# A written-out order for four engines: the pieces of one batch round stand in another order

## The reference

```python
# layer 0 and layer 2: chunks of 64 columns, 8 heads of 16, keys = queries' source = ctx
out = chunk_attn(ctx, ctx, ctx, mask, W_in, b_in, W_out, b_out) + x
x   = (out - mean(out)) * rsqrt(var(out) + eps)          # over the row
# layer 1: 32 heads of 32 with 8 key/value heads, low-rank additions to every weight
x   = hidden + attention(hidden=x, traces=ctx)           # 128 rows x 128 keys
# layer 3: first three rows of the context are coordinates
idx = top_k(2 p.p - |p|^2 - |p|^2, 30)                   # 1024 x 1024 distances per batch
rel = pts[idx] - pts                                     # gathered neighbours
h   = three small layers with batch norm over all batches, on (rho, theta, phi) of rel
x   = x + sum_k softmax(h)_k * x[idx_k]
```

## Time and profile before

| | us |
|---|---|
| median of 3 runs | 6556.02 (6547.49 to 6559.64) |
| the profiled execution, its own time | 6548.45 |
| its span, first to last instruction | 6546.7 |
| PE busy in the span | 6073.3 (93%) |
| DVE busy | 5841.3 (89%) |
| ACT busy | 4481.8 (68%) |
| POOL busy | 3099.7 (47%) |
| mean granted TensorE clock | 0.965 of full |

### The profile page before, as it was taken

One profiled execution on the slowest core, in us unless ns is written; L12 is line 12 of the kernel. 1 busy time (PEld: TensorE's weight loads), 2 busy tenths in 40 slices (PEclk: granted clock), 3 DMA queues, 4 the chain that ended last, 5 costly groups with the idle time before them and its releaser, 6 DMA issues.

```text
span 6546.7 us, 207457 instructions
## 1 busy us (share of the span) xinstructions
PE 6073.3 (93%) x79430; PEld 4398.2 (67%) x79430; DVE 5841.3 (89%) x8381; ACT 4481.8 (68%) x10453; POOL 3099.7 (47%) x3527
## 2 busy tenths in 40 slices
PE   8999999999999999999999999999999795999999
PEld 4666666666666666666666666666666333888888
DVE  6999999999999999999999999999998678888887
ACT  4777777667777776777677777666776146777776
POOL 3555555555555555555555555555555200333221
PEclk9999999999999999999999999999999897999999
DMA  4222222222222222222222222222223303322222
...
DMA packets 301388, 499.07 MB, mean 76 GB/s; under 512 B 103858, under 2 KB 217698, under 8 KB 299682
## 3 DMA queue, kind: packets, MB, share of 16 engines
...
## 4 chain that ended last, share of the span: by engine, by line
PE 58%; DVE 19%; issue 11%; DMA 5%; ACT 3%; POOL 2%; DVEq 0%; SPq 0%; POOLq 0%; ACTq 0%
PE PD L1183 7%; PE PD L718 5%; PE MISC L743 5%; DVE pd L1768 4%; PE SCB L1169 4%; PE SCA L1169 4%; DVE m L1758 4%; DMA gat<-low_scratch 4%; PE TP L904 3%; PE SCA L938 3%; DVE idx L1764 3%; DVE gat L1711 3%; PE TP L911 2%; PE TP L790 2%; PE SCB L815 2%
## 5 line engine op out<-in xcount | busy, mean ns | idle before, releaser
L1758 DVE MAX8 m<-pd 128x8 f32<-128x1024 f32 x1024 | 1234.0, 1220 | 121.0 <-issue 45.3
L1764 DVE FIND_INDEX8 idx<-m,pd 128x8 uint32<-128x1024 f32 x1024 | 1245.7, 1219 | 5.8 <-issue 5.6
L545 POOL TENSOR_TENSOR prod<-prod,hm 128x480 f32<-128x480 f32 x384 | 416.3, 1084 | 1255.7 <-ACT prod L1373 1224.0
L1768 DVE MATCH_REPLACE8 pd<-m,pd 128x1024 f32<-128x1024 f32 x768 | 927.3, 1209 | 0.0
L743 PEld LDWEIGHTS MISC<-ptab,gat 128*128 128x128 bf16 x23400 | 638.4, 97 | 242.3 <-DVE gat L1711 137.0
L1253 ACT ACTIVATE pd<-PD,xxcol 128x512 f32<-128x512 f32 x514 | 354.8, 690 | 636.5 <-PE PD L719 464.1
L743 PE MATMUL MISC<-ptab,gat 128*128 128x24 bf16 x23400 | 654.3, 174 | 119.7 <-DVE gat L1711 119.2
L2070 DVE TENSOR_TENSOR gat<-maskT,con 120x2048 f32<-120x2048 f32 x256 | 581.5, 2302 | 123.4 <-PE SCB L1169 97.5
L1352 ACT ACTIVATE S<-SCB,mx 128x64 f32<-128x64 f32 (+1 forms) x2560 | 590.4, 368 | 78.9 <-DVE mx L1780 78.9
L718 PE MATMUL PD<-arena 128*128 128x512 f32 x1028 | 558.8, 626 | 49.5 <-ACT pd L1253 44.4
L1352 ACT ACTIVATE S<-SCA,mx 128x64 f32<-128x64 f32 (+1 forms) x2560 | 585.5, 415 | 12.7 <-DVE mx L1780 12.1
(11 more groups left out here) (274 smaller groups left out, 14397.3 us busy)
## 6 DMA issues: line engine op xcount, KB each, us to landing
gat<-low_scratch SPq DMA_DIRECT2D x396, 640.0 KB, 4.0
...
```

The lines of the kernel that those rows point to most:

```text
L1758: V.max(m, buf[:, :]).then_inc(found, 1)
L1764: last = V.max_index(idx[:, t, 8 * r:8 * r + 8], m, buf[:, :])
L1768: V.match_replace(buf[:, :], m, buf[:, :], -3.0e38).then_inc(found, 1)
```

## The change

In `rounds(i)` of PE, ACT, DVE and POOL the same pieces stand in another order; SP's list is as it was. No piece is added or taken out, only the eleven steps of the searches are cut at other places. The diff, cut to its core (POOL and DVE whole, PE and ACT their beginnings and ends):

```diff
--- before.py
+++ after.py
@@ -610,26 +610,26 @@
 
 pool.wait_ge(split_ready, i + 1)
 consume(i, 0)
-consume(i, 1)
-consume(i, 2)
 sides(i, 0)
 sides(i, 1)
+consume(i, 1)
 sides(i, 2)
 sides(i, 3)
+blend(0, X1)
+consume(i, 2)
 consume(i, 3)
-blend(0, X1)
+tangents(i, 0)
 consume(i, 4)
 consume(i, 5)
-tangents(i, 0)
 consume(i, 6)
 consume(i, 7)
 consume(i, 8)
 blend(1, X0)
 tangents(i, 1)
+turn(i)
+norm_parts(i + 1)
 consume(i, 9)
 consume(i, 10)
-turn(i)
-norm_parts(i + 1)
 consume(i, 11)
 indices()
 table()
@@ -940,128 +940,128 @@
     if h:
         last.then_inc(oproj_ready, 1)
 
+keys(0)
+distance(i, 1, 0, (pd_evac, i * 16 + 2))
+queries(0)
 chunk_values(0)
-keys(0)
-queries(0)
-split(i)
-distance(i, 1, 0, (pd_evac, i * 16 + 2))
-turn_context()
 distance(i, 1, 1, (pd_evac, i * 16 + 3))
 scores(0, 0)
 scores(0, 1)
-fill(i, 0, MISC)
 x3_half(i, 0, (pd_evac, i * 16 + 4))
+split(i)
+x3_half(i, 1, (tab_done, i * 2 + 1))
+turn_context()
 turn_probs(0, 0)
 turn_probs(0, 1)
+distance(i, 2, 0, (tab_done, i * 2 + 2))
+scores(0, 2)
+weigh(0, 0)
+fill(i, 0, MISC)
+weigh(0, 1)
+turn_probs(0, 2)
+turn_probs(0, 3)
 fill(i, 1, MISC)
-weigh(0, 0)
-weigh(0, 1)
-x3_half(i, 1, (tab_done, i * 2 + 1))
-scores(0, 2)
-turn_probs(0, 2)
-fill(i, 2, MISC)
-outputs(0)
-turn_probs(0, 3)
-distance(i, 2, 0, (tab_done, i * 2 + 2))
 weigh(0, 2)
 weigh(0, 3)
-fill(i, 3, MISC)
 scores(0, 3)
+outputs(0)
+distance(i, 2, 1, (pd_evac, i * 16 + 5))
 turn_probs(0, 4)
 turn_probs(0, 5)
-distance(i, 2, 1, (pd_evac, i * 16 + 5))
+fill(i, 2, MISC)
 weigh(0, 4)
+weigh(0, 5)
+outputs(1)
+turn_probs(0, 6)
 queries(1)
-turn_probs(0, 6)
-weigh(0, 5)
 turn_probs(0, 7)
-outputs(1)
 outputs(2)
-full_values()
 weigh(0, 6)
 weigh(0, 7)
-full_keys()
+full_values()
 outputs(3)
 distance(i, 3, 0, (pd_evac, i * 16 + 6))
 project(0)
+full_keys()
+chunk_values(1)
+distance(i, 3, 1, (pd_evac, i * 16 + 7))
+fill(i, 3, MISC)
...
-fill(i, 10, MISC)
-turn_probs(2, 5)
-turn_probs(2, 6)
-norms(i + 1, 0, (pd_evac, i * 16 + 16))
-turn_probs(2, 7)
 weigh(2, 4)
 weigh(2, 5)
+norms(i + 1, 0, (pd_evac, i * 16 + 16))
 weigh(2, 6)
+norms(i + 1, 1, (xx_evac, i * 3 + 4))
 weigh(2, 7)
-norms(i + 1, 1, (xx_evac, i * 3 + 4))
-fill(i, 11, MISC)
 outputs(10)
+norms(i + 1, 2, (xx_evac, i * 3 + 5))
 outputs(11)
-norms(i + 1, 2, (xx_evac, i * 3 + 5))
+fill(i, 10, MISC)
 project_full(0)
 project_full(1)
+fill(i, 11, MISC)
 distance(i + 1, 0, 0, (xx_evac, i * 3 + 6))
 distance(i + 1, 0, 1, (pd_evac, i * 16 + 17))
 
@@ -1422,133 +1422,133 @@
     act.wait_ge(v_ready, i * 2 + 2)
     act.dma_start(ctx[:, :], ctx_in[(i + 1) % NB, :, :]).then_inc(ctx_ld, 16)
 
-value_evacuate(0)
 key_evacuate(0)
 expand(0, 0)
+distance(i, 1, 0)
+expand(0, 1)
+query_evacuate(0)
+distance(i, 1, 1)
+value_evacuate(0)
+expand(0, 2)
+x3_half(i, 0)
 split_evacuate(i)
-distance(i, 1, 0)
-query_evacuate(0)
-expand(0, 1)
-distance(i, 1, 1)
-expand(0, 2)
 exponentials(0, 0)
 exponentials(0, 1)
+x3_half(i, 1)
+evict(0, 0)
+evict(0, 1)
+context_evacuate()
+exponentials(0, 2)
+exponentials(0, 3)
 pick(0)
-evict(0, 0)
-context_evacuate()
-evict(0, 1)
-x3_half(i, 0)
-exponentials(0, 2)
-pick(1)
-exponentials(0, 3)
-x3_half(i, 1)
+expand(0, 3)
 evict(0, 2)
-expand(0, 3)
 evict(0, 3)
-pick(2)
+distance(i, 2, 0)
 exponentials(0, 4)
 exponentials(0, 5)
-distance(i, 2, 0)
-output(0)
+pick(1)
 evict(0, 4)
 evict(0, 5)
+output(0)
 exponentials(0, 6)
 exponentials(0, 7)
 evict(0, 6)
+output(1)
+store_rows()
 evict(0, 7)
-store_rows()
+output(2)
 distance(i, 2, 1)
-pick(3)
-output(1)
...
 angles(act, i)
+norms(i + 1, 2)
 output(10)
 output(11)
+pick(10)
 pick(11)
-norms(i + 1, 2)
 distance(i + 1, 0, 0)
 deviation(1)
 distance(i + 1, 0, 1)
@@ -1819,88 +1819,100 @@
 
 search(0, 0, 1)
 mask_bias()
-search(0, 1, 8)
+search(0, 1, 4)
+search(1, 0, 1)
+search(0, 4, 5)
 front(0, 0)
+search(0, 5, 6)
+search(1, 1, 2)
 front(0, 1)
+search(0, 6, 7)
+search(1, 2, 3)
+search(0, 7, 9)
 onehot(i, 0)
 onehot(i, 1)
-search(0, 8, 10)
-search(1, 0, 2)
 onehot(i, 2)
-search(1, 2, 3)
+search(1, 3, 4)
+search(0, 9, 11)
+front(0, 2)
+normalise(0)
+search(1, 4, 5)
+normalise(1)
+front(0, 3)
+search(1, 5, 8)
+normalise(2)
+search(1, 8, 11)
+search(2, 0, 1)
+normalise(3)
+search(2, 1, 3)
 onehot(i, 3)
-normalise(0)
-front(0, 2)
-search(1, 3, 6)
-search(0, 10, 11)
 onehot(i, 4)
+search(2, 3, 4)
 onehot(i, 5)
-front(0, 3)
-search(1, 6, 8)
-normalise(1)
-search(1, 8, 9)
-normalise(2)
-search(1, 9, 10)
-search(2, 0, 4)
-search(1, 10, 11)
-normalise(3)
-search(2, 4, 6)
+search(2, 4, 7)
+moments(X1)
+scaled(0)
+search(2, 7, 10)
+search(3, 0, 1)
 onehot(i, 6)
-search(2, 6, 11)
-moments(X1)
-search(3, 0, 1)
-scaled(0)
-search(3, 1, 4)
+search(2, 10, 11)
 front(1, 0)
-search(3, 4, 7)
+search(3, 1, 6)
 front(1, 1)
-divide(i)
-search(3, 7, 8)
+search(3, 6, 7)
+search(4, 0, 1)
+search(3, 7, 9)
+search(4, 1, 3)
+front(1, 2)
+search(4, 3, 4)
+search(3, 9, 10)
+search(4, 4, 6)
+search(3, 10, 11)
+normalise(4)
+search(4, 6, 7)
 onehot(i, 7)
 onehot(i, 8)
-search(4, 0, 2)
-search(3, 8, 9)
-search(4, 2, 3)
-front(1, 2)
-search(4, 3, 6)
-normalise(4)
-search(4, 6, 7)
-search(3, 9, 11)
-search(4, 7, 9)
+onehot(i, 9)
 front(1, 3)
 normalise(5)
-onehot(i, 9)
-search(4, 9, 11)
+search(4, 7, 8)
+normalise(6)
+search(4, 8, 9)
+divide(i)
+search(4, 9, 10)
 onehot(i, 10)
+search(4, 10, 11)
 front(2, 0)
-search(5, 0, 4)
-normalise(6)
+search(5, 0, 1)
+front(2, 1)
 normalise(7)
-search(5, 4, 6)
-onehot(i, 11)
-front(2, 1)
+search(5, 1, 7)
 front(2, 2)
-search(5, 6, 9)
-search(6, 0, 1)
+search(5, 7, 9)
+front(2, 3)
 search(5, 9, 10)
 normalise(8)
 search(5, 10, 11)
 normalise(9)
-front(2, 3)
-search(6, 1, 4)
-search(7, 0, 3)
+search(6, 0, 2)
+onehot(i, 11)
+search(6, 2, 4)
 normalise(10)
+search(7, 0, 1)
 normalise(11)
-search(7, 3, 5)
+search(7, 1, 4)
 search(6, 4, 6)
-search(7, 5, 9)
-search(6, 6, 7)
-search(7, 9, 10)
-search(6, 7, 11)
-search(7, 10, 11)
+search(7, 4, 6)
+search(6, 6, 8)
+search(7, 6, 7)
+search(6, 8, 10)
+search(7, 7, 8)
+search(6, 10, 11)
 full_residual()
 moments(X0)
+search(7, 8, 9)
 scaled(1)
+search(7, 9, 11)
 assert chain[0] == DVE_STEPS, chain[0]
 
             with dve.Fori(0, NB // 2) as pair:
```

149 lines of the change are left out of this document (75 added, 74 removed).

## The result

The changed kernel takes 6583.64 us (median of 6 runs, 6564.88 to 6607.20), the kernel before 6557.09 us (6 runs, 6547.49 to 6563.20): a ratio of 1.0046, 95% interval 1.0032 to 1.0060. It is slower, by 27 us from median to median and by 30 us by the ratio, where 26 us faster were forecast. The time lies inside the range, near its upper end, and the sign is wrong.

What follows compares the result with a forecast made beforehand. The prediction took DVE to bound a round, PE nearly as close. Its terms summed to -0.9 us a round, -29 us over 32, with 3 us added for the ends: -26 us, 6556 to 6530 us; range 6478 to 6590.

Steps and rivals of the forecast that it cites:

- Term 1: VectorE's searches: ten fewer largest-eight or taking-out steps directly followed by a dependent one, at 0.23 us: -2.3 us a round.
- Term 2: Round's end: a search step covers 0.7 us of waits, but scaled(1) waits about 0.7 us after ScalarE's table load: 0.
- Terms 3 and 4: One-hots: 0 to 2 wait and stretch more, +0.8 us a round; the later ones fall in POOL's gaps, -0.8 us.
- Term 5: Waits of 1.3 us at moments(X1) instead of 0.5, +0.8 us a round, and at scaled(0), +0.4 us.
- Term 6: Small stalls at front(2, 0) and normalise(7), where PE and DVE meet within 0.3 us: +0.2 us a round.
- against a round without the turn of the loop: Basis of the walk: per-round effects reckoned on a round without a loop turn, summing to -0.9 us, times 32.
- DVE is the bound of a round, with PE and the chains some microseconds behind: Whole round: DVE bounds it, 145.3 us of DVE and 146.2 us of PE; PE and ACT/POOL chains some microseconds behind.
- The second rival: Turn of the round: PE becomes the bound if its waits are 2 us more than 4.3: +38, 6594 us; chance 0.20.

Runs made afterwards that it cites:

- Experiment 3: Kernel before, only the searches' steps dealt out anew, 29 dependent neighbours down to 16: 6577.98 us, 1.0034.
- 1: Changed kernel with the first steps of search(1) put back behind those of search(0) in VectorE's list: 6584.22 us, 1.0039.
- 9: Changed kernel with TensorE's split and ScalarE's split_evacuate put forward, behind distance(i, 1, 1) and its copy: 6551.46 us, 0.9989.
- 10: Kernel of 9 with VectorE's first steps of search(1) a little later, 20 dependent neighbours instead of 19: 6537.31 us, 0.9959.
- 11: Changed kernel with four rounds to a turn of the loop instead of two: 6547.82 us, 0.9987.
- 12: Kernel before with four rounds to a turn of the loop instead of two: 6530.76 us, 0.9952.
- 6: Kernel before with project_full summing 6 of its 8 parts, 3.6 us less TensorE time a round: 6529.22 us, 0.9957.
- 17: Kernel before with three unread products ahead of chunk_values(0) at the head of each TensorE round: 6650.82 us, 1.0158.
- 5: Changed kernel with project_full summing 6 of its 8 parts, 3.6 us less TensorE time a round: 6555.51 us, 1.0005.
- experiment 15: Changed kernel with a milder split move, later first search(1) steps, and search(2, 7, 8) between moments(X1) and scaled(0): 6580.83 us, 1.0040.
- experiment 13: Kernel of 10 with five unread products ahead of split(i) on TensorE, where it waited for GpSimd: 6637.48 us, 1.0124.

## Why the prediction was wrong, by its own steps

*Term 1, ten dependent neighbours fewer: right.* The idle time ahead of an index step's load, in both kernels (before first):

```profile
L1764 DVE MATCH_VALUE_LOAD idx<-m,pd 128x8 f32 x992 | 84.4, 85 | 88.2 <-DVE m L1758 8.2
```

```profile
L1764 DVE MATCH_VALUE_LOAD idx<-m,pd 128x8 f32 x984 | 81.6, 83 | 42.2 <-DVE m L1758 7.6
```

46 us in 31 rounds, 0.15 us for each of the ten, and the 0.09 us by which an independent instruction starts before the largest-eight step has ended. Experiment 3, with 13 fewer, has it in whole rounds: the shortest takes 150.8 us, before 153.1; 13 at 0.23 us would be 3.0.

*Term 2, the end of the round:* right, `scaled(1)` waits 0.74 us in the row; forecast 0.7.

*Terms 3 and 4, the one-hots:* too dear. One-hot 0 starts 17.8 us into a round that doesn't follow a turn (forecast 18):

```profile
879.20 0.89 DVE L1711 TENSOR_SCALAR gat<-gat,con 128x2560 bf16<-128x2560 bf16 x1 [0.50 <-DMA gat<-low_scratch]
881.39 0.95 DVE L1711 TENSOR_SCALAR gat<-gat,con 128x2560 bf16<-128x2560 bf16 x1 [1.30 <-DMA gat<-low_scratch]
882.98 1.18 DVE L1711 TENSOR_SCALAR gat<-gat,con 128x2560 bf16<-128x2560 bf16 x1 [0.64 <-DMA gat<-low_scratch]
```

They wait about as long as thought, but aren't stretched to 1.8 us, although GpSimd's `high` runs through all three:

```profile
871.45 14.25 POOL L607 TENSOR_SCALAR hm<-hif 128x240 bf16<-128x240 f32 x8 [0.16 <-issue]
```

Why they were stretched before and are hardly so now stays open. Waits +33 us, durations -49 us (334.7 for 384.1): -0.5 us a round where 3 and 4 together had 0.

*Term 5:* right. `moments(X1)` waits 1.05 us (forecast 1.3), `scaled(0)` 0.36:

```profile
913.63 1.28 DVE L1809 BATCH_NORM_STATS2 bst<-X 128x6 f32<-128x512 f32 x2 [1.05 <-POOL X L602]
...
915.63 0.16 DVE L1817 RECIPROCAL rstd<-std 128x1 f32<-128x1 f32 x1 [0.36 <-ACT std L1385]
```

*Term 6, small stalls:* too small. The normalise steps wait 31.7 us in all instead of 4.8, `full_residual` 14.8 instead of 4.1: +1.2 us a round; the row maxima wait 0.3 us less. That is +0.9 us, forecast +0.2.

*The step that failed is the first one: "against a round without the turn of the loop".* The walk was made for that round and multiplied by 32. But half of the rounds follow a turn. The wait of `search(1, 0, 1)` for ScalarE there, 41.3 us in all, 2.8 us each, is in no term; one-hot 0 comes 3.5 us later there as well (median 21.0 us into the round, 17.5 in the others). By whole rounds the change makes +2.2 us in those behind a turn and +0.1 in those that end in one (157.2 for 154.9, 156.0 for 156.0), together 37 us over 16 turns, the 34 us of the profiled spans. Against the forecast of -0.9 that is 3.1 us missed in each round behind a turn, 50 us in 16, and 1.0 us in each of the others, 16 us: three quarters of the miss lie where no walk was made, and the rest, in the rounds that were walked, is not much more than the 0.7 us a round that term 6 missed.

The two engines say the same. VectorE's own time fell by 2.2 us in rounds of both kinds, as terms 1, 3 and 4 have it; its idle time rose by 4.4 us behind a turn (9.5 to 13.9) and by 2.1 us in the others (10.7 to 12.8), the first two rounds left out. What is shown: the place (traces), that a search step moved back doesn't cure it (1), that putting the split forward brings 32 us and 46 with the search step (9, 10). That fewer turns help the changed kernel by 36 us and the other by 26 (11, 12) points the same way, within the noise. That the table load behind the wait for `keys(0)` is 1.28 us of ScalarE's lateness stands in the rows; what it is worth in time isn't shown, since a list that puts `value_evacuate(0)` first again was not run.

*"DVE is the bound of a round, with PE and the chains some microseconds behind"* was too strong as well: 3.6 us off TensorE's round are worth 0.8 us (6), and 3.6 us on it cost 3.1 (17). The second rival (slower, 6594 us) had the sign and nearly the size, but by luck. Its condition, waits of TensorE for exponentials and one-hots 2 us beyond the 4.3, isn't met: they come to 98 us, 3.2 us a round (4.3 with the waits at the same lines that the profile puts down to issue), and before they were 4.3, not some 9. And it put the loss at the round's end, where experiments 5 and 6 don't find it. What grew is TensorE's own time, for the same products: 147.2 to 149.4 us behind a turn, 145.3 to 146.4 in the other rounds.

*TensorE's clock* was in no term. Within the rounds the trace shows 297 us at half clock before and 457 after; 160 us more at half clock are 80 us of TensorE's work, 2.5 us a round at the most, enough for that growth. Whether that costs, two rounds of the changed kernel say, both without a turn ahead. TensorE, 13.4 us into each; up to there their starts agree to 0.01 us:

```profile
2130.79 1.12 PE L880 MATMUL SCA<-con,S 128*128 128x128 f32 x4 [2.08 <-ACT S L1352]
...
2135.61 1.03 PE L862 MATMUL SCA<-sel 6*128 6x512 bf16 x2
2136.57 1.99 PE L869 MATMUL SCA<-kexp,reg 64*64 64x256 f32 x16
```

```profile
4324.49 0.66 PE L880 MATMUL SCA<-con,S 128*128 128x128 f32 x4 [2.08 <-ACT S L1352]
...
4329.16 0.60 PE L862 MATMUL SCA<-sel 6*128 6x512 bf16 x2
4329.69 1.09 PE L869 MATMUL SCA<-kexp,reg 64*64 64x256 f32 x16
```

After the same wait of 2.08 us the one (start 2117.38) goes at half clock for 13.7 us, the other (start 4311.09) for only 3.4 us, a little later. `scores(0, 2)` ends 21.2 us into the one and 19.7 us into the other. Over whole rounds of one place behind the turn, each microsecond of half clock goes with 0.2 to 0.5 us more of round (correlation 0.69 and 0.86 in the changed kernel, 0.98 and 0.97 in experiment 15, 0.53 and none in the kernel before). But the total alone doesn't order the kernels: experiments 9 and 10 have 481 and 444 us of it and are faster than the changed kernel, and experiment 13 has 375 us and is slower. Where it falls may matter more; no run varies that alone. How much of the 30 us is clock, and why it falls in one round and not in its twin, stays open. Experiment 15 doesn't price it either: its 28 us go with half clock at 60 to 80 us, but the total rose only from 440 to 478 us, and the new waits for scores stand beside it.
